# Loading the last stage's raw weights and first attention output inside attention, and opening that stage in quarters

## The reference

```python
mod = (_silu(c) @ wmod).reshape(4, 6, 1, -1)
sa, ca, ga, sb, cb, gb = (mod[:, i] for i in range(6))   # ga, gb kept at least 0.25 in size
h = _layernorm(x) * (1 + ca) + sa
x = x + ga * attention(h, W_kv_down, W_k_up, W_v_up, W_q, W_q_rope, W_k_rope, W_o)
h = _layernorm(x) * (1 + cb) + sb
x_prev = h shifted by one row
xr, xk = mu_r * h + (1 - mu_r) * x_prev, mu_k * h + (1 - mu_k) * x_prev
x = x + gb * sigmoid(xr @ W_r.T) * (square(relu(xk @ W_k.T)) @ W_v.T)
```

## Time and profile before

| | us |
|---|---|
| median of 3 runs | 3919.67 |
| lowest and highest | 3917.86, 3922.95 |
| profiled execution | 3919.98 |
| its span | 3918.3 |

### The profile page before, as it was taken

How to read it: one execution, slowest core, us unless ns; L and a number is a source line. 1 busy time by engine, 2 the same in 40 slices (tenths; PEclk the granted TensorE clock), 3 DMA queues, 4 the chain that set the end, 5 groups by cost and what they waited for, 6 DMA issues and landing times. The chain is left out here.

```text
span 3918.3 us, 56697 instructions
## 1 busy us (share of the span) xinstructions
PE 3643.2 (93%) x19808; PEld 2454.7 (63%) x19808; DVE 2844.3 (73%) x5454; ACT 1805.1 (46%) x3401; POOL 2444.0 (62%) x1145
## 2 busy tenths in 40 slices
PE   7999879999999999999999999999998699999998
PEld 3777645665665665656656666566564577777776
DVE  5777577777777777778777777777773577777776
ACT  2343335555555555555555555555554233333332
POOL 1333237677777787777777867777778355555555
PEclk8999989999999999999999999999999799999999
DMA  5789743463543634634436345344430311111110
GB/s 176 258 270 296 264 99 76 90 134 78 113 98 83 141 79 95 135 73 108 104 88 130 79 103 127 76 106 109 90 83 6 129 64 54 64 57 53 61 64 32
DMA packets 232267, 425.83 MB, mean 109 GB/s; under 512 B 25332, under 2 KB 26868, under 8 KB 231928
## 3 DMA queue, kind: packets, MB, share of 16 engines
q1 hardware_dynamic: 231992, 423.10, 41.5%
q10 hardware_dynamic: 64, 0.02, 0.0%
HBM read 300.86 MB, written 121.65 MB: 108 GB/s over the span
## 5 line engine op out<-in xcount | busy, mean ns | idle before, releaser
L831 ACT ACTIVATE att_probs<-att_ps_s 128x512 f32<-128x512 f32 (+3 forms) x2560 | 1316.4, 534 | 1153.9 <-PE att_ps_s L986 1058.3
L937 POOL TENSOR_TENSOR att_sum_g<-att_sum_g,att_probs 128x2048 f32<-128x2048 f32 (+3 forms) x384 | 1447.3, 3769 | 207.3 <-ACT att_probs L831 171.6
L867 DVE TENSOR_REDUCE att_piece_max<-att_ps_m 128x1 f32<-128x512 f32 x1536 | 973.1, 680 | 218.6 <-PE att_ps_m L971 215.6
L985 PE MATMUL att_ps_s<-att_q_a,att_k_a 128*128 128x512 f32 (+3 forms) x2560 | 962.2, 380 | 15.8 <-DMA att_q_b<-att_neg_max 15.7
L986 PE MATMUL att_ps_s<-att_q_b,att_k_b 65*128 65x512 f32 (+3 forms) x2560 | 942.5, 371 | 0.0
L971 PE MATMUL att_ps_m<-att_k_a,att_q_a 128*128 128x512 f32 (+3 forms) x1840 | 674.3, 391 | 72.6 <-DVE att_piece_max L867 36.1
L870 DVE CUSTOM_DVE_ANT_0 att_ps_m<-att_ps_m,mask_qk 128x128 f32<-128x128 f32 (+3 forms) x1024 | 489.5, 507 | 291.4 <-PE att_ps_m L971 281.0
L985 PEld LDWEIGHTS att_ps_s<-att_q_a,att_k_a 128*128 128x128 f32 x2560 | 491.5, 192 | 137.1 <-issue 61.6
L971 PEld LDWEIGHTS att_ps_m<-att_k_a,att_q_a 128*128 128x128 f32 x1840 | 348.2, 192 | 350.1 <-DVE att_piece_max L867 129.1
L992 PE MATMUL att_ps_o<-att_probs,att_v 128*32 128x512 f32 (+3 forms) x5120 | 549.4, 535 | 7.3 <-POOL att_probs L915 7.3
L986 PEld LDWEIGHTS att_ps_s<-att_q_b,att_k_b 65*128 65x128 f32 x2560 | 489.2, 191 | 68.0
(11 more groups left out here) (173 smaller groups left out, 5230.1 us busy)
## 6 DMA issues: line engine op xcount, KB each, us to landing
att_q_a<-s_q_hi SPq DMA_DIRECT2D x128, 256.0 KB, 6.4
att_q_a<-s_qr_hi SPq DMA_DIRECT2D x128, 256.0 KB, 7.2
prj_x_sb<-in_x_dram SPq DMA_DIRECT2D x16, 1024.0 KB, 5.4
s_q_hi<-prj_q_hi SPq DMA_DIRECT2D x16, 1024.0 KB, 4.4
s_q_lo<-prj_q_lo SPq DMA_DIRECT2D x16, 1024.0 KB, 6.5
s_k_hi<-prj_k_hi SPq DMA_DIRECT2D x16, 1024.0 KB, 4.5
s_k_lo<-prj_k_lo SPq DMA_DIRECT2D x16, 1024.0 KB, 6.5
s_v<-prj_v_sb SPq DMA_DIRECT2D x16, 1024.0 KB, 9.4
```

Source lines behind the costliest of these rows:

```text
L831: act.activation(probs[t % RING][:, hh, c0:CH], ps_s[(GH * t + hh) % SBANKS][:, c0:CH], ACT.Exp, scale=SCALE).then_inc(probs_ready, 1)
L867: dve.tensor_reduce(top, ps_m[:, bank, :], AX_X, ALU.max).then_inc(piece_taken, 1)
L937: pool.tensor_tensor(sum_g[:, :, c0:CH], sum_g[:, :, c0:CH], new, ALU.add).then_inc(sum_added, 1)
L985: mm(out[:, c0:CH], k_a[:, hh, i * P:(i + 1) * P], q_a[j][:, hh, c0:CH], start=True, stop=False)
```

## The change

Five loads move from the opening of `feedforward` into unit 15 of attention, where SP has no next operands to load: after the scores of chunk 0 the attention output of the first chunk, w_o and w_v, after those of chunk 1 w_r, after those of chunk 2 w_k. They land in the memory of operands that unit 15 has finished with (the queries of these chunks and `k_next`), under the names `raw_...`; `feedforward` keeps using attention's tiles, so that `att_k_a` in a row now holds both halves of w_o or w_r, `att_k_next` the high half of w_k, `att_v` the x of a chunk, and `att_q_a`, `att_q_b` the mixes.

In the opening the gates are loaded by sequence, that of sequence 0 first and the others last; x is loaded second, the second attention output without a wait. Attention output and w_o are cast in quarters, in turn; w_o's low half is made in quarters; POOL no longer waits for the gates first; PE makes the row blocks 0 and 1 of the projection between w_r and w_k, and 2 and 3 between w_k and w_v.

```diff
+def raw_views(nc):
+
+    with ExitStack() as ctx:
+        ctx.enter_context(nc.sbuf_tensor("under_raw", [P, GH * T + TCH * TB * P], F32))
+        names = ("w_o", "w_r", "w_v", "w_k", "att")
+        return {n: ctx.enter_context(nc.sbuf_tensor("raw_" + n, [P, NC, D], F32)) for n in names}
...
+            def load_for_last_stage(j):
+                wait_alone(sp, scores_ready, GH * (NSTEP * (NU - 1) + FIRST[j] + STEPS[j]), sp_mark)
+                if j == 0:
+                    wait_alone(sp, o_stored, 16 * (TCH * (NU - 2)), sp_mark)
+                    sp.dma_start(ops["raw"]["att"][:], scratch["o"].rearrange("(g n) p t -> n p g t", g=NG)[0]).then_inc(ops["att_in"], 16)
+                    load_weight(0)
+                    load_weight(3)
+                else:
+                    load_weight(j)
...
                     load_q(u + 1, 0)
+                else:
+                    load_for_last_stage(0)
                 store_o(u, 0)
                 place_max(u, 2)
...
+            def load_gate(b):
+                sp.dma_start(gate[:, b:b + 1, :, :], scratch["gate"][None, b:b + 1].broadcast_to([P, 1, 2, D])).then_inc(gate_rest if b else gate_in, 16)
-            load_weight(1)
-            load_weight(0)
-            sp.dma_start(att_f[:], att_v[0]).then_inc(att_in, 16)
-            load_weight(2)
+            load_gate(0)
             sp.dma_start(x_sb[:], x_v[0]).then_inc(x_in, 16)
-            sp.dma_start(gate[:], scratch["gate"][None].broadcast_to([P, NB, 2, D])).then_inc(gate_in, 16)
-            load_weight(3)
             sp.dma_start(mu[:, 0, :], dram["mu_r"].rearrange("(c p) -> p c", p=P), allow_slow_non_contiguous=True).then_inc(mu_in, 16)
             sp.dma_start(mu[:, 1, :], dram["mu_k"].rearrange("(c p) -> p c", p=P), allow_slow_non_contiguous=True).then_inc(mu_in, 16)
-            sp.wait_ge(att_lo, NG)
             sp.dma_start(att_f[:], att_v[1]).then_inc(att_in, 16)
+            for b in range(1, NB):
+                load_gate(b)
...
+            def output_weight_low(c):
+                dve.wait_ge(wo_hi, c + 1)
+                dve.tensor_tensor(w_o[1][:, c, :], w_raw[0][:, c, :], as_f32(w_o[0][:, c, :]), ALU.subtract).then_inc(wo_lo, 1)
+
...
-            weight_low(0)
+            for c in range(NC):
+                output_weight_low(c)
             weight_low(1)
+            dve.wait_ge(gate_in, 16)
+            attention_out(0, range(0, 2))
             weight_low(2)
-            dve.wait_ge(gate_in, 16)
-            attention_out(0)
+            attention_out(0, range(2, TB))
             layernorm(0)
             weight_low(3)
             normalise(0)
             carry(0, False)
             dve.wait_ge(mu_in, 32)
+            dve.wait_ge(gate_rest, 16 * (NB - 1))
             token_shift(0, lambda m: None)
...
-            act.copy(w_o[0][:], w_raw[0][:]).then_inc(w_hi, 1)
-            split_attention(0)
+            act.wait_ge(att_in, 16)
+            for g in range(NG):
+                act.copy(att[0][:, g, :], first_att[:, g, :]).then_inc(att_hi, 1)
+                act.copy(w_o[0][:, g, :], w_raw[0][:, g, :]).then_inc(wo_hi, 1)
+            act.wait_ge(att_lo, NG)
...
-            pool.wait_ge(gate_in, 16)
-            low_attention(0)
+            low_attention(0, first_att)
             residual(0)
             inv_std(0)
             low_attention(1)
+            pool.wait_ge(gate_in, 16)
+            pool.wait_ge(gate_rest, 16 * (NB - 1))
...
                     for c in range(NG):
+                        if not reuse and m == 0:
+                            pe.wait_ge(att_lo, c + 1)
+                            pe.wait_ge(wo_lo, c + 1)
...
+            turn_weight(1)
+            attention_out(0, False, range(0, 2))
+            turn_weight(2)
+            attention_out(0, False, range(2, TB))
+            turn_weight(3)
+            pe.wait_ge(w_lo, 3)
```

More of the change, by code:

```diff
@@ L644, in operand_loads, with attention @@
     return load_q_a, load_q_b, load_k_a, load_k_b, load_v, (heads, rotary)
-def attention(nc, keep, scratch, ops):
+def attention(nc, keep, scratch, ops, dram):
     with ExitStack() as ctx:
@@ L660, in attention @@
         probs = [sb(f"probs{i}", [P, GH, CH], F32) for i in range(RING)]
-        k_next = sb("k_next", [P, GH, CH], F32R)
+        k_next = ops["k_next"]
         sum_g = sb("sum_g", [P, GH, CH], F32)
@@ L762, in store_o, with load_weight @@
                 sp.dma_start(scratch["o"][TCH * u + j], o_sb[j % 2][:]).then_inc(o_stored, 16)
+            def load_weight(i):
+                name = ("w_o", "w_r", "w_k", "w_v")[i]
+                sp.dma_start(ops["raw"][name][:], dram[name].rearrange("(c p) n -> p c n", p=P)).then_inc(ops["w_in"][i], 16)
+            def load_for_last_stage(j):
[7 more added lines that the diff above has]
+                    load_weight(j)
             def body(u, nxt):
@@ L775, in body @@
                     load_q(u + 1, 1)
+                else:
+                    load_for_last_stage(1)
                 store_o(u, 1)
@@ L780, in body @@
                     load_q(u + 1, 2)
+                else:
+                    load_for_last_stage(2)
                 store_o(u, 2)
@@ L985, in scores @@
                 mm(out[:, c0:CH], k_a[:, hh, i * P:(i + 1) * P], q_a[j][:, hh, c0:CH], start=True, stop=False)
-                last = mm(out[:, c0:CH], k_b[:, hh, i * P:(i + 1) * P], q_b[j][:, hh, c0:CH], start=False, stop=True)
+                last = mm(out[:, c0:CH], k_b[:, hh, i * P:(i + 1) * P], q_b[j][0:2 * HD + 1, hh, c0:CH], start=False, stop=True)
                 last.then_inc(scores_ready, 1)
@@ L1040, in _, with feedforward @@
                     close_denominators(*CLOSE_AT[t])
-def feedforward(nc, keep, dram, scratch, out):
+def feedforward(nc, keep, dram, scratch, out, ops):
     with ExitStack() as ctx:
@@ L1049, in feedforward @@
         pair = lambda n, s: (sb(n + "_hi", s, F32R), sb(n + "_lo", s, F32R))
-        w_o, w_r, w_k, w_v = (pair(n, [P, NC, D]) for n in ("w_o", "w_r", "w_k", "w_v"))
+        w_o, w_r = ([ops["k_a"][:, k, :].rearrange("p (c n) -> p c n", c=NC) for k in two] for two in ((0, 1), (2, 3)))
+        w_k = ops["k_next"], sb("w_k_lo", [P, NC, D], F32R)
+        w_v = pair("w_v", [P, NC, D])
         mu = sb("mu", [P, 2, NC], F32)
@@ L1071, in feedforward @@
         xn = diff
-        w_raw = (diff, x1, x1_kept, gate_r)
+        w_raw = [ops["raw"][n] for n in ("w_o", "w_r", "w_k", "w_v")]
+        first_att = ops["raw"]["att"]
         kact = att
-        w_in = [sem(f"w_in_{a}") for a in "orkv"]
+        w_in, att_in = ops["w_in"], ops["att_in"]
         w_turned, w_hi, w_lo, mu_in, gate_in = (sem(n) for n in ("w_turned", "w_hi", "w_lo", "mu_in", "gate_in"))
-        att_in, x_in, y_stored = sem("att_in"), sem("x_in"), sem("y_stored")
+        wo_hi, wo_lo, gate_rest = sem("wo_hi"), sem("wo_lo"), sem("gate_rest")
+        x_in, y_stored = sem("x_in"), sem("y_stored")
         att_hi, att_lo = sem("att_hi"), sem("att_lo")
@@ L1496, in adaln_block @@
         }
+        raw = raw_views(nc)
         with ExitStack() as held:
@@ L1502, in adaln_block @@
                 projection(nc, keep, dram, scratch, prj, ops)
-            attention(nc, keep, scratch, ops)
-        feedforward(nc, keep, dram, scratch, out)
+            late_operands(nc, held, ops)
+            ops["raw"] = raw
+            attention(nc, keep, scratch, ops, dram)
+            feedforward(nc, keep, dram, scratch, out, ops)
 _INS = {
```

44 lines of the change are left out of this document (22 added, 22 removed).

## The result

| | before | with the change |
|---|---|---|
| median of 6 runs each, us | 3921.22 | 3896.48 |
| lowest and highest | 3916.99, 3923.27 | 3894.32, 3899.56 |
| profiled execution (span) | 3919.98 (3918.3) | 3897.63 (3895.9) |

The ratio is 0.9941, 95% interval 0.9929 to 0.9953: 18 to 28 us faster. The forecast was 3899.3 in 3895.5 to 3904.5.

What follows compares the result with a forecast made beforehand. The last stage's opening was bound by the gates' load, holding POOL and then PE for 17.59 us. From the 3919.67 us median, 20.4 us gained (middle of 21.5 and 19.2, less 0 in attention) gave 3899.3, range 3895.5 to 3904.5.

Steps and rivals of the forecast that it cites:

- Loads in attention, taken at 0: Unit 15 of attention: the five moved loads cost 0 to 8.8 us of PE stall, taken as 0.
- PE's and ACT's entry, taken 0.7 us after S: Opening of the last stage: PE and ACT start at 3037.5, SP's first issue there being at 3036.79.
- The collision: Opening: DVE's w_o quarters overlap POOL's attention-output subtractions, slowing both; low halves end at 3045.2, upper bound 3046.3.
- The clock: Opening, PE's matmuls: full clock gains 21.5 us, low clock 19.2; the middle, 20.4, was taken.
- The rival of the low clock through row blocks 0 and 1: Opening: PE's clock stays low there, or the collision reaches its upper bound; 3900.5 to 3903 us, chance 0.30 together.
- mu and the gates: Opening: needed at 3065.3, in before 3056, 9 us slack; the rival of a late landing, 3907 us, had chance 0.06.
- S at 3036.8: SP's first issue of the last stage stays at 3036.8; later than 3040 would be wrong.
- Later chunks slower with the same code: Last stage after the opening: cost taken as 0; slower chunks with unchanged instructions would show the forecast wrong.

Runs made afterwards that it cites:

- e5: The changed kernel plus six unused 1 MB transfers behind the first three moved loads in unit 15; median 3901.25 us, ratio 0.9954 to the kernel before.
- e6: The changed kernel with DVE's first memset moved behind row blocks 0 and 1; median 3897.20 us, ratio 0.9931 to the kernel before.
- e7: The changed kernel with DVE's memset moved late and DVE, not POOL, making the first attention output's low halves; median 3892.31 us, ratio 0.9925 to before.
- e8: e7 with w_v's low half made in quarters, two ahead of the normalising and two behind; median 3885.98 us, ratio 0.9917 to the kernel before.
- e2: The changed kernel with the five loads back in the opening, new order and quarters kept; median 3905.78 us, ratio 0.9976 to the kernel before.
- e4: The changed kernel with row block 0 of the projection ahead of w_r's transposes, block 1 behind; median 3899.70 us, ratio 0.9957 to the kernel before.
- e1: The changed kernel with early loads kept but w_o whole and the projection after w_r's and w_k's transposes; median 3901.92 us, ratio 0.9961 to before.

## Why the prediction held

- **Loads in attention, taken at 0.** Right. The interval from the maxima to S lies at 120.5 to 121.8 us with and without them, and e5 shows what guards it.
- **PE's and ACT's entry, taken 0.7 us after S.** They come at S + 0.06 and S + 0.16. It moved nothing, since DVE and POOL set the next step.
- **The collision.** DVE's last quarter was to end 8.4 us after S and ends at 8.1; the pace of 1.68 us was to be 1.6 to 1.7. The Trainium skill, "SBUF — State Buffer", section "SBUF: two separate sides", says that DVE with two SBUF inputs and a GpSimd instruction that reads SBUF share a port pair by an exclusive lock and not by splitting its rate. The trace comes near it and does not meet it: a pair takes 1.68 us, 1.6 in e6, where the two one after the other would take 1.83 (0.60 of e7's spacing and POOL's 1.23 alone); what hides the difference isn't known. e7 shows what leaving POOL out returns.
- **The clock.** Of the terms of the sum only this one, sized off, moved the result. The sum had two ends, 21.5 us at the full and 19.2 at the low clock, and I took the middle. The clock rose 3.0 us after S, and the opening came out at 40.94 - 19.48 = 21.46, the full end to 0.1 us. What counted was only that the clock was up by S + 8.2, when PE stopped waiting for DVE; in e5 to e8, which open with the same transposes, it was up by S + 4.6. The rival of the low clock through row blocks 0 and 1 did not occur in the change, though e2 and e4 had it in part. The rule weighed there (the Trainium skill, "TensorE: Matmul & The Clock Gate", Part 4, transposes don't count as activity) doesn't fit the change: PE had been idle for 7.49 us and up to 3036 did nothing in this stage but transposes, and the clock went from 0.51 to 1.00. It doesn't fit e2 either, where the rise at 3048.5 followed w_r's sixteen transposes and nothing else. But sixteen transposes don't always bring the rise: in e1 PE turned w_r from S + 0.1 on as in the change, and the clock stayed at 0.50 until 3049.0, S + 11.3, near the end of w_k's transposes. So the rows I had could not settle which end holds, and the middle was a hedge between them and not a reading.
- **mu and the gates.** No wait; mu 23 us early where the sum had 9, because the sum put all 4 MB ahead of mu and only 1.5 MB stood there, and the two issues took 0.5 and 0.85 us where the second had taken 6.07 before.
- **S at 3036.8.** It was 3032.95, a miss of this sign, of which 2.86 us were there before the first moved load and are no effect of it.
- **Later chunks slower with the same code** was named as another sign of being wrong, and by the letter it is there: 835.5 us behind the transposes, before 832.6. Ten kernels with this loop spread over 820.8 to 837.1, so it shows no cost of the change and rules out none of a few us.

From 3899.3 to the median of 3896.48 are 2.8 us. The middle between the clock's ends accounts for 1.1. The other 1.7 are not explained by a step; they are less than the 5 us over which six executions of one kernel lie. Set against the six-run median of the kernel before, 3921.22 and not the 3919.67 the forecast started from, the gain is 24.7 us, of which the opening shows 21.5; that the total lay so near the forecast is partly the scatter of the two medians.

**Left open: what makes the loop's time scatter.** The rest took 820.8 to 837.1 us in ten kernels with one loop. PE's waits in 760 us of it for ACT's sigmoid, in the change and in e2:

```profile
PE ffn_ps_ffn L59 <- ACT ffn_gate_r L1358: 37.3, 13, 3.3
```

```profile
PE ffn_ps_ffn L59 <- ACT ffn_gate_r L1362: 16.8, 13, 3.3
```

The granted clock there was 0.96 in the change and 0.97 in e2. In all ten kernels these waits are between 17.6 us (e2, the shortest rest) and 42.0 (e6, the longest), each over the 760 us from 3090 on (the two stretches above start some 26 us later), and go with the rest though not strictly: 20.2 in e4 with 827.5 us, 33.2 in e7 with 827.4. I suspect that the place in an iteration at which the clock falls sets these waits, but the share of low clock doesn't order the kernels (before 0.98 with 832.6 us, e2 0.97 with 820.8), and no run was made that fixes it. It is argued, not shown.

## What to carry to other kernels

At a passage between two stages, first look for waits placed ahead of work that doesn't need them: one moved wait gave 7.8 of 21.5 us here. Then count what the queue must carry in the opening; a load moved into the stage before is free as long as the queue is empty again when that stage's small, urgent rows come, and costs its whole delay from there on, with the fall of TensorE's clock during the stall on top (e5: the row 9.9 us late, attention some 11.4 us longer). Where such a change is judged end to end, compare also the stretch itself in the trace: here two kernels with the same opening, the change and e5, agree in it within 0.01 us (19.48 and 19.47) while the loop, whose instructions are the same, varies by 16.

## What the runs showed of the hardware

- An 8 KB transfer behind 6 MB more on the same queue landed 11.7 us after its issue, 1.8 without.
- The clock stood at 1.00 through threes of matmuls with gaps of 0.7 us when it had risen before them (the change), and at 0.50 through threes of the same pace when it had not (e4) or had fallen again (e2). Five kernels open with the same sixteen transposes and the projection behind them, and the rise comes 3.0 us after S in the change, 3.4 in e5, 4.1 in e6, 4.4 in e7 and 4.6 in e8; why isn't known.
- POOL's subtraction of 128x512 takes 1.23 us alone and DVE's 0.60 back to back. Side by side a pair takes 1.6 to 1.7 us, so that the slower engine's help saved nothing: two on DVE alone take 1.2.
